# Vision tower kernel: rope projections and linear experts split 128 + 64, unread products in three kinds of phases, two tiles' second products ahead of the list

## The reference

```
h = tok(x)
h = h + L0_attn(layernorm(h));  h = h + L0_ffn(layernorm(h))   # linear experts, 8 of 192 x 192, top 2
h = h + L1_attn(layernorm(h));  h = h + L1_ffn(layernorm(h))   # fake-quantised attention; T5 stack, 4 layers
h = h + L2_attn(layernorm(h));  h = h + L2_ffn(layernorm(h))   # rope attention; 16 experts, top 2
h = h + L3_attn(layernorm(h));  h = h + L3_ffn(layernorm(h))   # partial rope attention; 16 experts, top 8
```

```
# L0_ffn: probabilities of the chosen two, linear experts
out = sum_e gate[t, e] * (x[t] @ expert_w[e].T + expert_b[e])
# L2_attn, L3_attn: 12 heads of 16 numbers, sequences of 16 tokens
q, k = rope(x @ wq.T + bq), rope(x @ wk.T + bk);  v = x @ wv.T + bv
out = softmax(q k^T / 4 (causal in L2)) v @ wo.T + bo
# L1_ffn, layers 1 and 3: dense feed-forward plus 8 experts, top 2
y = relu(n @ wi) @ wo2;  y = y + moe_ffn(n)
```

## Time and profile before

| | us |
|---|---|
| Median of three runs | 1668.78 |
| Lowest and highest | 1668.5, 1670.88 |
| Profiled execution | 1679.46 |
| Its span on the core | 1677.7 |

### The profile page before, as it was taken

The page is one execution under the profiler, slowest core; times in us unless marked ns, Lnnn a source line. Parts: engine busy times, 40 slices in busy tenths (PEclk is TensorE's granted clock), DMA queues, the critical chain, the costliest instruction groups (busy, mean ns, idle before and its releaser), DMA issues. The chain is left out here.

```text
span 1677.7 us, 35609 instructions
## 1 busy us (share of the span) xinstructions
PE 1385.0 (83%) x14474; PEld 1084.8 (65%) x14474; DVE 633.4 (38%) x1654; ACT 473.0 (28%) x1254; POOL 504.7 (30%) x650
## 2 busy tenths in 40 slices
PE   6377854999998999499999899848649995876997
PEld 6164432788885899388878589714539984453756
DVE  2544664333344222234334422155451113453434
ACT  0420052433443111234344111114213332421121
POOL 0010174222232265322232236424126653330000
PEclk9677965999999999799999899968559997956999
DMA  5010111000000542300000343210034543010000
GB/s 130 0 30 13 48 42 57 35 2 2 9 12 20 200 144 93 130 2 2 2 11 12 132 151 126 93 45 4 27 129 124 181 169 105 4 59 1 29 29 19
DMA packets 40118, 101.75 MB, mean 61 GB/s; under 512 B 15856, under 2 KB 26228, under 8 KB 34864
## 3 DMA queue, kind: packets, MB, share of 16 engines
q0 software_dynamic: 18480, 58.56, 10.2%
q1 hardware_dynamic: 19744, 38.52, 7.3%
q10 hardware_dynamic: 1728, 2.36, 0.5%
HBM read 137.96 MB, written 11.50 MB: 89 GB/s over the span
## 5 line engine op out<-in xcount | busy, mean ns | idle before, releaser
L1266 PE MATMUL bank<-t_ew,t_hg 128*128 128x192 f32 x552 | 97.2, 327 | 0.0
L1266 PEld LDWEIGHTS bank<-t_ew,t_hg 128*128 128x128 f32 x552 | 88.7, 190 | 0.2
L1298 ACT ACTIVATE t_hg<-bank 128x384 f32<-128x384 f32 x92 | 40.1, 488 | 166.6 <-PE bank L1254 105.0
L1513 DVE SCALAR_TENSOR_TENSOR h<-bank,cw,h 128x192 f32<-128x192 f32 x128 | 53.5, 418 | 88.2 <-PE bank L1436 71.4
L337 PE MATMUL bank<-ident,rows 128*96 128x128 f32 x96 | 21.9, 423 | 70.6 <-DVE rows L320 70.6
L1294 ACT ACTIVATE l_hg<-bank,l_ew 128x128 f32<-128x128 f32 x186 | 51.3, 374 | 101.7 <-PE bank L1254 51.5
L2091 POOL TENSOR_SCALAR t_rstd<-t_ssq 128x1 f32<-128x1 f32 x64 | 12.2, 190 | 217.4 <-ACT t_junk L1927 217.2
L1250 PE MATMUL bank<-t_xgT,t_ew 128*128 128x128 f32 x552 | 69.9, 276 | 4.7 <-DVE t_xgT L1330 4.3
L1848 PE MATMUL bank<-t_wo,t_ctx 128*128 128x192 f32 x384 | 71.0, 335 | 0.9 <-ACT t_ctx L1944 0.9
L1250 PEld LDWEIGHTS bank<-t_xgT,t_ew 128*128 128x128 f32 x552 | 67.2, 192 | 6.8 <-DVE t_xgT L1330 5.9
L1158 POOL DMA_INDIRECT t_ew<-in_t_moe,source x46 | 47.5, 1032 | 79.6 <-DVE t_og L1339 34.8
(11 more groups left out here) (354 smaller groups left out, 3091.1 us busy)
## 6 DMA issues: line engine op xcount, KB each, us to landing
t_qkv<-in_t_wqkv SPq DMA_DIRECT2D x9, 576.0 KB
t_wo<-in_t_wo SPq DMA_DIRECT2D x8, 576.0 KB
w<-in_l_w SPq DMA_DIRECT2D x8, 576.0 KB, 4.6
wA<-in_t_wqkv SPq DMA_DIRECT2D x2, 1728.0 KB
patches<-in_patches SPq DMA_DIRECT2D x8, 384.0 KB, 9.5
rows_in<-rows SPq DMA_DIRECT2D x24, 128.0 KB, 1.7
t_wi<-in_t_wi SPq DMA_DIRECT2D x3, 576.0 KB
t_gg<-rows_out ACTq DMA_DIRECT2D x8, 192.0 KB, 4.4
```

The costliest lines, as they stand in the source:

```text
L1266: mm = pe.matmul(k.bank[6 + b % 2][:, 0:DIM], k.hg[b % 2][:, m, :], w[:, SPLIT + m * DIM:SPLIT + (m + 1) * DIM], start=(m == 0), stop=(m = ...
L1298: ins = act.activation(k.hg[b % 2][:, o:FC:2, :], hidden(b, o)[:, 0:FC // 2 * P].rearrange("p (m q) -> p m q", q=P), func)
L1513: ins = dve.scalar_tensor_tensor(out, src, k.cw[:, tile, bass.ds(col, 1)], out, ALU.mult, ALU.add)
```

## The change

It has five edits.

`idle_products` is new: `n` products of the identity with `k.blk`, 384 columns of float32, into a bank that is started anew before anyone reads it. It is called in every norm phase (four before the first transpose, one after the last), in the rope attention (one before each tile's score, four after tile 1's score), and at the start of the pair phase (three).

The linear experts and the rope projections take the split form, with the weights laid out for it on the host. For the rope projection the two 64-row products of a job are its plain and its swapped half; for the values they are two neighbouring tiles. In the linear experts they are two neighbouring pairs of experts, and the semaphore `turned` rises for both pairs after the second.

The norm phases before them and the first router are therefore called with `split=True`.

In the choice phase the second products of tiles 0 and 1 stand before the list, and the banks of the second products are taken in the order 6, 7, 5, since bank 5 holds the ranks.

```diff
+def idle_products(pe, k, bank, n):
+    for _ in range(n):
+        pe.matmul(bank[:, 0:HPU * P], k.ident[:], k.blk[:].rearrange("p j q -> p (j q)"), start=True, stop=True)
...
 norm_phase, tensor:
+            idle_products(pe, k, k.bank[7], 4)
             for t in range(NT):
...
                 mm.then_inc(k.turned, 1)
+            idle_products(pe, k, k.bank[7], 1)
...
 compact_attention_phase, tensor:
+                    idle_products(pe, k, s_bank(t), 1)
                     score(pe, t, s_bank(t)).then_inc(k.scores, 1)
+                if s == 1:
+                    idle_products(pe, k, k.bank[6], 4)
...
 rope_projection_phase, tensor, for each job:
-                for s in range(2):
-                    for c in range(2):
-                        mm = pe.matmul(k.bank[2 * (i % 4) + s][0:CH, :],
-                                       w[:, 2 * which + s, c, m * CH:(m + 1) * CH],
-                                       k.xT[:, c, n * HALF:(n + 1) * HALF], start=(c == 0), stop=(c == 1))
-                    mm.then_inc(k.turned, 1)
+                for s in range(2):
+                    col = (2 * group + s) * CH
+                    pe.matmul(k.bank[2 * (i % 4) + s][0:CH, :], w[:, col:col + CH], k.xTs[:, 0, toks],
+                              start=True, stop=False)
+                for s in range(2):
+                    col = 4 * DIM + group * CH
+                    pe.matmul(k.bank[2 * (i % 4) + s][0:CH, :], w[halves[s], col:col + CH], k.xTs[halves[s], 1, toks],
+                              start=False, stop=True).then_inc(k.turned, 1)
...
 and for the values, two tiles at a time:
+                for o in range(2):
+                    pe.matmul(k.bank[t + o][:, 0:DIM], k.xTs[:, 0, (t + o) * P:(t + o + 1) * P], w[:, 6 * DIM:7 * DIM],
+                              start=True, stop=False)
+                for o in range(2):
+                    pe.matmul(k.bank[t + o][:, 0:DIM], k.xTs[halves[o], 1, (t + o) * P:(t + o + 1) * P],
+                              w[halves[o], 7 * DIM:8 * DIM], start=False, stop=True).then_inc(k.turned, 1)
...
 linear_experts_phase, tensor, for each pair p of a tile:
-                        for c in range(2):
-                            mm = pe.matmul(k.bank[i % 8][:, 0:2 * DIM], k.xT[:, c, t * P:(t + 1) * P],
-                                           w[:, c, (p - 1) * 2 * DIM:p * 2 * DIM], start=(c == 0), stop=(c == 1))
-                    mm.then_inc(k.turned, 1)
+                        pe.matmul(k.bank[i % 8][:, 0:2 * DIM], k.xTs[:, 0, toks], w[:, (p - 1) * 2 * DIM:p * 2 * DIM],
+                                  start=True, stop=False)
+                        if p % 2 == 0:
+                            for o in range(2):
+                                half = slice(o * REST, (o + 1) * REST)
+                                col = (n_e + p - 2) * DIM
+                                mm = pe.matmul(k.bank[(i - 1 + o) % 8][:, 0:2 * DIM], k.xTs[half, 1, toks],
+                                               w[half, col:col + 2 * DIM], start=False, stop=True)
+                                mm.then_inc(k.turned, 1)
...
 t5_pair_phase, tensor:
+            idle_products(pe, k, score_bank, 3)
             for s in range(-1, units + 2):
...
 t5_choice_phase:
-    out_banks = k.bank[5:8]
+    out_banks = (k.bank[6], k.bank[7], k.bank[5])
...
+            second(0)
+            second(1)
             list_places(pe, k, nb, list_bank)
-            for t in range(NT):
+            for t in range(2, NT):
                 second(t)
```

More of the change, by code:

```diff
@@ L715, in _ @@
         def _(pe):
+            halves = [slice(o * REST, (o + 1) * REST) for o in range(2)]
             for i, (which, m, n) in enumerate(jobs):
@@ L718, in _ @@
                     pe.wait_ge(k.evacuated_v, 2 * (i - 3))
+                toks, group = slice(n * HALF, (n + 1) * HALF), 2 * which + m
                 for s in range(2):
-                    for c in range(2):
-                        mm = pe.matmul(k.bank[2 * (i % 4) + s][0:CH, :],
-                                       w[:, 2 * which + s, c, m * CH:(m + 1) * CH],
-                                       k.xT[:, c, n * HALF:(n + 1) * HALF], start=(c == 0), stop=(c == 1))
-                    mm.then_inc(k.turned, 1)
-            for t in range(NT):
-                if t % 2 == 0:
-                    pe.wait_ge(k.evacuated_v, 2 * (len(jobs) - 3 + t // 2))
-                for c in range(2):
-                    mm = pe.matmul(k.bank[t][:, 0:DIM], k.xT[:, c, t * P:(t + 1) * P], w[:, 4, c, :],
-                                   start=(c == 0), stop=(c == 1))
-                mm.then_inc(k.turned, 1)
+                    col = (2 * group + s) * CH
[5 more added lines that the diff above has]
+                              start=False, stop=True).then_inc(k.turned, 1)
+            for t in range(0, NT, 2):
+                pe.wait_ge(k.evacuated_v, 2 * (len(jobs) - 3 + t // 2))
+                for o in range(2):
[4 more added lines that the diff above has]
+                              w[halves[o], 7 * DIM:8 * DIM], start=False, stop=True).then_inc(k.turned, 1)
         @block.vector
@@ L1358, in _ @@
             for t in range(NT):
+                toks = slice(t * P, (t + 1) * P)
                 for p in range(pairs + 1):
@@ L1365, in _ @@
                     else:
[L1366 to L1369 removed]
+                        pe.matmul(k.bank[i % 8][:, 0:2 * DIM], k.xTs[:, 0, toks], w[:, (p - 1) * 2 * DIM:p * 2 * DIM],
[7 more added lines that the diff above has]
+                                mm.then_inc(k.turned, 1)
+                    if p == 0:
+                        mm.then_inc(k.turned, 1)
                     i += 1
@@ L2279, in build @@
         with stage() as st:
-            we = tensor(st, "l0_we", [CH, 2, 8 * DIM])
-            norm_phase(k, k.h, 1e-5, loads=[(we[:], a["l0_we"]), (k.bout[0:8, :], a["l0_be"])])
-            router_phase(k, 8, "probs", k.before[0], True, True)
+            we = tensor(st, "l0_we", [P, 12 * DIM])
+            norm_phase(k, k.h, 1e-5, split=True, loads=[(we[:], a["l0_we"]), (k.bout[0:8, :], a["l0_be"])])
+            router_phase(k, 8, "probs", k.before[0], True, True, split=True)
             linear_experts_phase(k, we, 8, loads=[(k.wA[0:CH, 0:2 * 3 * DIM].rearrange("p (c n) -> p c n", c=2),
@@ L2378, in build @@
                 ctxT = [tensor(st, f"l{level}_ctxT{i}", [CH, 2, P]) for i in range(2)]
-                norm_phase(k, k.h, 1e-5, loads=[(wA6, a[f"l{level}_w"]), (wo[:], a[f"l{level}_wo"]),
+                norm_phase(k, k.h, 1e-5, split=True, loads=[(wrope, a[f"l{level}_w"]), (wo[:], a[f"l{level}_wo"]),
                                                 (k.bias[:], a[f"l{level}_bv"])])
-                rope_projection_phase(k, wA6, 1 + 4 * (level - 2), level - 2, qT, kT, kx, vx)
+                rope_projection_phase(k, wrope, 1 + 4 * (level - 2), level - 2, qT, kT, kx, vx)
                 narrow_heads_attention(k, qT, kx, vx, k.near[:, 3 - level, :], ctxT, wo, k.h, k.bias,
@@ L2573, in lay_out @@
         w = {c: i[f"L{lv}_attn_" + ("w" if low else "W") + c] for c in "qkvo"}
-        mats = [w["q"].T, swap_halves(w["q"]).T, w["k"].T, swap_halves(w["k"]).T, w["v"].T]
-        a[f"l{lv}_w"] = np.stack([k_major(m) for m in mats], axis=1)
+        groups = [m[:, c * CH:(c + 1) * CH] for x in "qk" for c in range(2) for m in (w[x].T, swap_halves(w[x]).T)]
+        values = w["v"].T
+        a[f"l{lv}_w"] = np.concatenate([split_columns(np.concatenate(groups, axis=1), CH), values[:P],
+                                        np.concatenate([values[P:], values[P:]])], axis=1)
         a[f"l{lv}_wo"] = k_major(w["o"].T)
```

9 lines of the change are left out of this document (4 added, 5 removed).

## The result

On the chip of the profile above, the changed kernel took **1649.2 us** (median of four runs, 1646.09 to 1651.06) against 1669.83 for the kernel before (four runs, 1668.5 to 1672.64): **ratio 0.9847, 95% interval 0.9816 to 0.9878**. On a second chip, where the kernel before took 1698.5 us, the ratio was 0.9855 (0.9827 to 0.9883). So the change makes the kernel 1.5% faster, some 25 us, where the prediction had 37: the sign was right, and a third of the gain is missing. (The two medians alone differ by 20.6 us, the profiled executions by 28.4.) The median lies 1 us above the range of 1619 to 1648; the ratio times 1668.8 gives 1643, inside it.

A forecast was written before the change was run, and what follows sets the result against it. TensorE's clock, low after gaps or thin work, and its work or waits were taken to bound most phases. Terms summed to -36.8 us on the profiled 1679.5, scaled to 1668.8 - 36.6 = 1632 us, range 1619 to 1648.

The forecast's parts named there:

- Part 1: Two choice phases: second products of tiles 0 and 1 ahead of the list fill TensorE's wait, -12.7 us.
- Part 2: Linear experts: split blocks save 0.24 us each, -3.6 us in all.
- Part 3: Rope projections: split blocks save 0.46 us each, -2.4 us a level, -4.8 us for both.
- Part 4: Eight norms: unread products raise the clock, so transposes and copies end sooner, -5.4 us.
- The rule against part 4: Norms: the skill says transposes don't engage the full clock, so they couldn't hold it; priced as rival C.
- rival C: Norms and what follows: transposes don't hold the clock, most of that gain is lost, 1643 us; chance 0.08.
- Part 5: Starts behind norms: rope projections begin at full clock, -4.3 us; routers, -1.0 us.
- Part 6: Two pair phases: three unread products at the start raise the clock earlier, -2.0 us together.
- Part 7: Two rope attentions: cold opening, then tiles every 3.5 us at full clock, -1.5 us each, -3.0 us.
- B: Rope attentions: one or both stay at the low clock, 1646 or 1659 us; chance 0.12.
- D: Norms and attentions: TensorE stays at 1.2 GHz despite the products, so slower, about 1690 us; chance 0.03.
- A: Whole kernel: the forecast itself, 1621 to 1643 us; chance 0.62.

The follow-up runs named there:

- e5: The kernel before with only the choice phases' edit, second products of tiles 0 and 1 ahead of the list: 1689.8 us, ratio 0.9923.
- a0: The changed kernel itself, unaltered, run again on the second chip: 1673.51 us, ratio 0.9855 to the kernel before.
- e4: The changed kernel without any unread product, keeping the split forms and the choice phase's order: 1679.88 us, ratio 0.9882 to the kernel before.
- e3: The changed kernel without the norm phases' unread products: 1684.1 us, ratio 0.9903 to the kernel before.
- e9: The changed kernel, rope attention products moved to three behind score 2, one per tile from tile 3, one in each of the last two steps: 1663.95 us, ratio 0.9789.
- e10: Like e9, but also without the three unread products ahead of each pair phase: 1664.17 us, ratio 0.9778 to the kernel before.
- e8: The changed kernel, rope attention products moved to three behind score 2 and one per tile from tile 3: 1665.62 us, ratio 0.9807.
- e7: The changed kernel without the unread product ahead of each rope attention score, keeping the four behind the second score: 1672.34 us, ratio 0.9827.
- e6: The changed kernel without the four unread products behind the second rope attention score, keeping one ahead of each score: 1676.37 us, ratio 0.9832.

## Why the prediction was right or wrong, point by point

The profiled executions differ by 1679.46 - 1651.06 = 28.4 us. By phases of the two profiles (us):

| part | forecast | measured | from, to |
|---|---|---|---|
| 1 choice | -12.7 | -12.1 | 34.49 to 28.40; 34.66 to 28.63 |
| 2 linear experts | -3.6 | -3.8 | 50.58 to 46.80 |
| 3 and 5, rope projections | -9.1 | -10.7 | 36.78 to 30.86; 35.60 to 30.85 |
| 4 norms | -5.4 | -6.0 | mostly 5.29 to between 4.1 and 4.7, from ScalarE's root on |
| 5 routers | -1.0 | +0.6 | 14.68 to 16.43; 31.64 to 30.76; 9.46 to 9.14 |
| 6 pair phases | -2.0 | +1.7 | 244.88 to 245.83; 245.10 to 245.87 |
| 7 rope attentions | -3.0 | +4.5 | 36.95 to 39.2; 37.5 to 39.8 |
| all of these | -36.8 | -25.8 | |

What is left, -2.6 us, is the sum of larger gains and losses in phases that the change doesn't touch (in level 0: output projection -2.9, attention -1.6, projection +1.3). In the first two the kernel before has a stretch at 0.50 that the changed kernel has not. The attention's is there in e5 too, and in none of the twelve profiles of kernels with the split products; what moves it is open. (The terms of part 5's routers add up to -0.9, not -1.0.) The missing 11 us are part 7 with 7.5, part 6 with 3.7 and the routers with 1.6, less 1.9 in the parts that gave more.

**Part 1 right**, in place and size, and e5 shows it alone. The DMAs did not become late. **Part 2 right**: of the 0.24 us gained a block all was there. A tile took 5.18 us (from 148.79 to the same instruction of the next tile, 153.97), less than the 5.25 of the best case. Against it the clock rose 7.1 us into the phase, before 5.4; in a0, where it rose after 5.5, the phase took 46.0 us. The linear experts' split blocks in the changed kernel, timeline:

```profile
148.79 1.56 PE L1384 MATMUL bank<-l_we,xT 128*128 128x384 f32 x4
150.28 0.92 PE L1390 MATMUL bank<-l_we,xT 64*128 64x384 f32 x4
151.12 1.56 PE L1384 MATMUL bank<-l_we,xT 128*128 128x384 f32 x4
```

151.12 - 148.79 = 2.33 us, the number taken from the earlier trace rows. **Part 3 right**: 30.9 us with a warm start. The fairest pair for the split alone is level 3 in the kernel before and in e4: in both the clock fell to 0.50 for 3.4 us just behind the start, and they took 35.60 and 32.45 us. That is 3.15 us where 2.4 was taken, an estimate from two profiles. The rest of the 10.7 us, 4.4, is the warm start, for which part 5 took 4.3.

**Part 4 right, with its range of late rises.** Six of the eight are 0.6 to 1.2 us shorter. In level 2's the products ran 5.46 us at 0.50 and reached past the point where the first transpose was due; that norm gained 0.07. The norm that writes its rows gained 0.25 and gave nothing on, as said: from VectorE's first normalised tile to the router's first product it is 7.30 us, before 7.31.

**The rule against part 4.** The rows first: in the changed kernel the clock reads 1.00 from 1095.70 on, through twelve of the sixteen transpose instructions, the unread product behind them and the seam, to 1129.90; and the earlier trace rows had it rise out of pure transposes. They don't raise it in time everywhere: in e3, with transposes alone in its norms, both rope projections and the quantised projection began with 3.0 to 6.0 us at 0.50. The Trainium skill's sentence on transposes (TensorE: Matmul & The Clock Gate, Part 4) would have made rival C true; rival C's price, 10.2 us by its terms, is by chance near what is missing, but no part of it was paid in norms or rope projections.

**Part 5, routers: wrong by 1.6 us.** The clock was 0.50 from 122.9 to 146.8, so the first router paid for its split form and got little back. The same phase took 14.7 us in the kernel before and 15.8 in e5, 15.7 to 16.7 in the kernels with the split router and the norms' products, and 17.3 and 16.5 in e3 and e4: the price is about 1 us. The gain at the two other routers isn't firm either: level 3's took 9.1 to 10.0 us with the products, 9.5 and 9.4 in the kernel before and e5.

**Part 6 wrong.** The start did gain: the first score of the first pair came 12.73 us after the start, before 13.66. But in the second pair the clock rose only at 689.5, 8.9 us after its start (before 9.0), and in the middle of the first one it dropped once:

```profile
464.20:467.60 3.40, 2.45 (x125) 2.12 (x114) 1.54 (x3) 0.85 (x5) 1.08 (x2) 1.00 0.00 0
467.60:471.10 3.50, 3.50 (x22) 3.28 (x23) 1.41 (x4) 0.75 (x3) 0.83 (x1) 0.51 0.02 5
```

Ahead of the drop TensorE had 2.45 us of work in 3.40, most of it products on 32 rows or 32 columns of the array. Of the 28 pair phases some have no such drop, some one or two, at 25 to 27 or at 179 to 194 us behind the start. The three of 250 us (a0, e9 and e10, with the pair products and without) have both, so a gain of 1 us at the head of a 245 us phase is under its scatter.

**Part 7: right in the middle, wrong at both ends.** The step that failed is "following the queue, value 0 starts at 9 us ... a last stretch 1.7 shorter at full clock". Point by point for level 2 and level 3: value 0 at 9, measured 10.0 and 10.7; tile 4's bias at 16.0, measured 17.0 and 17.7; three more biases at 3.5 us each, measured 3.74 and 3.72; last bias to end 9.0 us, measured 10.95 and 10.98, where the kernel before needed 10.7 and 11.4 at 0.50. That makes 3.7 and 4.3 us, the whole miss of this part, and half of it is the tail: I let the full clock last to the end of a phase whose last two steps have no score, no unread product and a wait for VectorE. The size was wrong as well: with the full clock to the end, in e9 and e10, the same stretch, with two unread products in it, took 9.6 to 10.2 us and not 9.0. The opening I had priced in the right way but too low. The clock rose 5.4 and 8.3 us in and not after 4, and a single unread product between two scores moved the next start by 1.55 us at 0.50, where 1.28 was taken; in a row they took 1.3 to 1.4 (eight instructions in 5.46 us). And I should have asked whether it had to be paid at all: TensorE waits there for the first probabilities anyway, and e8 and e9 put three products into that wait, with the first value product at 5.95 us in three of their four attentions and at 6.78 in the one that opened at 0.50.

**The rivals.** B (attention stays at 0.50) didn't happen; its cause did in e7. D didn't happen. C, E and F neither. A's own band, 1621 to 1643, holds the time only by the ratio, at its edge. No rival said what did happen, a middle at full clock whose gain is lost at both ends; only the bounds of part 7 hold it. With part 7 wrong at both ends, the total is as near as it is because parts 1 to 4 came true, helped by 1.9 us that they gave beyond their terms and 2.6 us that no part had.

## What to carry to other kernels

Work that is there only to raise a clock belongs where its engine waits anyway: behind the instructions that others wait for, never ahead of them. A product ahead of each of the first scores, and four more, held the first value product back by 4 to 5 us where it came after 6 (3.8 us when level 2 of a0 is set against that of e8, which opened as cold), more than the full clock gave back in the tiles behind. And it must reach to the end of the phase, since a tail of thin steps is where the clock falls; ask of each edit not only what the middle of a phase gains, but what its first and last step pay.

## What the runs showed of the hardware that was not expected

In e7 TensorE was busy 25.27 of 27.00 us and the granted clock stayed at 0.50; in e9 it was busy 25.90 of 29.80 us and the clock stayed at 1.00. What TensorE did differently is one full-array unread product per tile among the same 32-column and 32-row ones. The Trainium skill (TensorE: Matmul & The Clock Gate, Part 1) says that the gate goes by how busy the PE has been recently. By the busy share in these rows e7 should have had the 1.00 and e9 the 0.50, so they don't agree with it if busy is what the profile counts as busy. Nor does such a product in each tile always bring the clock up: in e6's level 3 it was there and the clock stayed at 0.50 through 9.96 busy us of 10.20.

One unread product took 1.6 us at the start of level 2's attention at 0.50 (1.62 and 1.65 us for its two instructions), but 0.81 us at 1.00. And the clock can rise late although TensorE does nothing but full-array products: in level 2's norm 5.46 us of them ran at 0.50 before it rose at 1095.70, 6.1 us after they began, while in other norms the same products had it up before the first transpose. What sets that the profile doesn't show; it is why one and the same phase takes 4.1 us in one profile and 5.2 in another.
